# Post-LN transformer layer on one core: scores over all 128 array rows, heads' outputs to columns by DMA, and a new order of steps

## The reference

```python
qkv = (x @ Wqkv + bqkv)                      # 16 heads of width 16
scores = einsum('bhnqd,bhnkd->bhnqk', qb, kwin) / 16     # blocks of 128 queries, 384 keys
mask = (abs(kpos - qpos) <= 128) & (kpos >= 0) & (kpos < S)
attn = softmax(where(mask, scores, -1e30))
x = layernorm(x + (attn @ vwin) @ Wout + bout)
W1q, W2q = ternary(W1), ternary(W2)          # -1, 0 or 1
x = layernorm(x + relu(x @ W1q.T + b1) @ W2q.T + b2)
```

## Time and profile before

| | |
|---|---|
| median of 3 runs | 1186.8 us (1184.37 to 1189.89) |
| profiled execution, time | 1187.86 us |
| profiled execution, span | 1186.1 us |
| mean granted TensorE clock | 0.924 of 2.4 GHz |
| DMA moved | 81.49 MB |

### The profile page before, as it was taken

One profiled execution on the slowest core, in us unless ns is written; L12 is line 12 of the kernel. 1 busy time (PEld: TensorE's weight loads), 2 busy tenths in 40 slices (PEclk: granted clock), 3 DMA queues, 4 the chain that ended last, 5 costly groups with the idle time before them and its releaser, 6 DMA issues.

```text
span 1186.1 us, 23520 instructions
## 1 busy us (share of the span) xinstructions
PE 1056.2 (89%) x8132; PEld 771.9 (65%) x8132; DVE 859.3 (72%) x2934; ACT 613.3 (52%) x1258; POOL 518.8 (44%) x824
## 2 busy tenths in 40 slices
PE   4778899999989899998989999898989999897966
PEld 3444676766767576676767666676767667675755
DVE  3975777778787777778777777877777787777333
ACT  4154554655455564556455555545655554555421
POOL 2124353544535445463535445453535445344430
PEclk9677899998989999898999989898998989898889
DMA  5835255434354443444344534424554342442000
GB/s 169 108 54 92 28 82 82 68 70 73 58 75 68 83 73 76 61 80 65 56 82 73 88 61 78 75 37 82 82 82 68 69 74 57 57 69 56 1 19 18
DMA packets 56999, 81.49 MB, mean 69 GB/s; under 512 B 7729, under 2 KB 27697, under 8 KB 56882
## 3 DMA queue, kind: packets, MB, share of 16 engines
q1 hardware_dynamic: 56882, 80.00, 40.3%
HBM read 20.19 MB, written 8.39 MB: 24 GB/s over the span
## 4 chain that ended last, share of the span: by engine, by line
PE 77%; DVE 13%; issue 4%; POOL 2%; ACT 2%; DMA 1%; SPq 0%; POOLq 0%; DVEq 0%; ACTq 0%
PE shared L484 18%; PE st_a L459 13%; PE shared L503 12%; PE shared L595 11%; PE shared L582 10%; DVE mx L812 5%; PE st_b L459 5%; PE shared L578 3%; PE shared L564 3%; DVE oT_lo L859 2%; POOL ln_rstd L1007 1%; PE shared L543 1%; PE mx L475 1%; DVE qk_lo L839 1%; DVE rmax L812 1%
## 5 line engine op out<-in xcount | busy, mean ns | idle before, releaser
L812 DVE CUSTOM_DVE_ANT_0 mx<-mx,band 128x384 f32<-128x384 f32 (+1 forms) x1024 | 480.1, 514 | 187.0 <-PE mx L475 182.6
L670 ACT ACTIVATE probs<-st_a 128x384 f32<-128x384 f32 (+1 forms) x384 | 202.0, 526 | 371.3 <-PE st_a L459 367.7
L475 PE MATMUL mx<-k_stack,q_stack 48*128 48x384 f32 (+1 forms) x1024 | 273.0, 369 | 8.0 <-DMA k_stack<-qk_lo 3.9
L973 POOL TENSOR_SCALAR_AFFINE_SELECT probs<-probs 128x512 f32<-128x512 f32 (+1 forms) x256 | 128.8, 527 | 317.5 <-ACT probs L670 316.3
L670 ACT ACTIVATE probs<-st_b 128x384 f32<-128x384 f32 (+1 forms) x384 | 200.8, 523 | 0.0
L459 PE MATMUL st_a<-q_stack,k_stack 50*128 50x384 f32 (+1 forms) x512 | 186.9, 406 | 3.1 <-ACT probs L670 2.4
L475 PEld LDWEIGHTS mx<-k_stack,q_stack 48*128 48x128 f32 x1024 | 165.7, 201 | 13.2 <-DVE rmax L812 8.7
L503 PE MATMUL shared<-probs,v_aug 128*32 128x384 f32 (+1 forms) x2048 | 161.2, 445 | 0.7 <-DVE x L902 0.7
L459 PEld LDWEIGHTS st_a<-q_stack,k_stack 50*128 50x128 f32 x512 | 90.3, 197 | 104.2 <-issue 63.5
L812 DVE DVE_READ_ACCUMULATOR2_ANT rmax<- 128x1 f32 x1024 | 144.5, 141 | 0.0
L459 PE MATMUL st_b<-q_stack,k_stack 50*128 50x384 f32 (+1 forms) x512 | 143.2, 320 | 0.0
(11 more groups left out here) (107 smaller groups left out, 1965.3 us busy)
## 6 DMA issues: line engine op xcount, KB each, us to landing
q_stack<-qk_hi SPq DMA_DIRECT2D x128, 128.0 KB, 4.3
k_stack<-qk_hi SPq DMA_DIRECT2D x128, 128.0 KB, 5.2
x_raw<-in_xT SPq DMA_DIRECT2D x16, 512.0 KB, 5.7
q_stack<-qk_lo SPq DMA_DIRECT2D x64, 128.0 KB, 3.9
k_stack<-qk_lo SPq DMA_DIRECT2D x64, 128.0 KB, 5.5
y<-in_x SPq DMA_DIRECT2D x16, 512.0 KB, 6.1
out<-x SPq DMA_DIRECT2D x32, 256.0 KB, 2.1
probs<-in_w2T SPq DMA_DIRECT2D x1, 1024.0 KB, 10.6
```

The lines of the kernel that those rows point to most:

```text
L475: mm = pe.matmul(PMX[i % N_MAX][:, col:col + n], SQ[rows, hd, W * m:W * m + W], SK[rows, hd, k0:k0 + n], start=True, stop=True)
L670: act.activation(PR[:, v % 2, g // 2, lo:lo + n], PST[i % 2][:, 0:n], ACT.Exp, scale=SCALE) \
L812: mx = dve.tensor_tensor_reduce(ps, ps, band, 1.0, -3e38, ALU.add, ALU.max, RMAX[:, g, m:m + 1])
L973: pool.affine_select(out=pr_before, in_=pr_before, compare_op=ALU.is_ge, fill=0.0, base=0, pattern=[[0, n], [1, W]], channel_multiplier=-1)
```

## The change

- `scores` and `max_scores` use the array's rows 0 to 127 and 0 to 111. `SK` becomes two stacks, each with zeros where the other pair of quads has its q rows; the negated maxima and ones move to rows 124 to 127. Scores and maxima no longer lie in different halves.
- A stack transfer also waits for the maxima of quad v-2, and scores also wait for the stack of the quad two ahead. Scores get three banks, shared work two; `nmt` uses a maxima bank, and the next max unit in it waits for ScalarE's copy.
- `ut` and the `ot` transposes go. `columns` copies the even rows of `U` (o) to `OC` and the odd rows (its sums, 16 times each) to `SC` with two DMAs for each quad. A step `od` takes the reciprocal of 128x512 sums and multiplies, twice in a row: VectorE both reciprocals and one product, GpSimd the other product.
- The bias matmul of `f1` goes: ScalarE makes relu with bias in two instructions into `U` or `H32`, then a third copies to `HID[0]`; the low part comes from there, by VectorE, in one of four by GpSimd.
- First layer norm in two halves; three of four x1 tiles on ScalarE. `SIDE`, `LAG` and the weaving change; SP's order is the table `TRANSFERS`.

```diff
+SIDE = [
+    ["nmt", ("ot", 0), ("qk", 0), "pva", "pvb", ("vp", 0), ("qk", 1), ("od", 1)],
+    [("ot", 1), ("vp", 1), ("qk", 2), ("op", 0), ("ln1", 0), ("ln1", 1), ("op", 1), "nmt", ("ln1", 2), ("x1", 0),
+     ("x1", 1), ("ln1", 3), ("qk", 3), ("xs", 0), "pva", "pvb", ("x1", 2)],
+    [("x1", 3), ("x1t", 0), ("x1t", 1), "nmt", ("f1", 0, 0), ("f1", 0, 1), ("f1", 0, 2), ("f1", 0, 3), "pva",
+     "pvb", ("f2", 0)],
+    [("ln2", 0), ("xs", 1), ("f1", 1, 0), ("f1", 1, 1), ("od", 0), ("f1", 1, 2), ("ln2", 1), ("f1", 1, 3),
+     ("f2", 1), ("ln2", 2), "nmt", ("ln2", 3), "pva", "pvb", "xr"],
+BANKS = (3, 3)
+REST_ON_POOL = (1,)
+X1_ON_DVE = (0,)
+SCORES_AT = (0.31, 0.94)
+MAXIMA_AT = (0.47, 0.89)
+TRANSFERS = (('maxima', 0), ('stack', 3), ('columns', 0), ('stack', 0), ('x', 0), ('maxima', 1), ('columns', 1), ('maxima', 2), ('residual', 0), ('stack', 1), ('columns', 2), ('stack', 2), ('store', 0), ('maxima', 3), ('columns', 3), ('store', 1))
+LAG = {"ln1": 1, "ln2": 0, "qk": 0, "od": 1, "ot": 2, "x1t": 0, "f1": 1, "op": 0, "f2": 0}
+        units = [((i + SCORES_AT[0]) / UNITS * total * SCORES_AT[1], "scores", i) for i in range(UNITS)]
+        units += [((i + MAXIMA_AT[0]) / UNITS * total * MAXIMA_AT[1], "max", i) for i in range(UNITS)]
+                if not (first and v < 2):
+                    sp.wait_ge(s_mxf, 12 * (4 * r + v - 2) + 12)
+                    if v < 2 or stages(at)[2]:
+                        pe.wait_ge(s_stk[(v + 2) % 4], 96 * (b + v // 2) + 96)
-                    mm = pe.matmul(PST[i % 2][:, col:col + n], SK[rows, hd, W * m:W * m + W],
-                                   SQ[rows, hd, q0:q0 + n], start=True, stop=True)
+                    mm = pe.matmul(PST[i % N_SCORE][:, col:col + n], SK[c][:, hd, W * m:W * m + W],
+                                   SQ[:, hd, q0:q0 + n], start=True, stop=True)
-                rows = slice(64 * c, 64 * c + 48)
+                rows = slice(0, 112)
+                if i == NMT_AT[(v + 2) % 4] and not (first and v == 0):
+                    pe.wait_ge(s_nmt, 4 * r + v)
+                sp.dma_start(OC[rows, i, :], U[0:P:2, :]).then_inc(s_uin, 16)
+                sp.dma_start(SC[rows, :], U[1:P:2, :]).then_inc(s_uin, 16)
-                        pe.matmul(ps, B1[:, P * f:P * f + P], ONES2[:, :], start=True, stop=False)
+                    for k, f in enumerate((2 * p, 2 * p + 1)):
+                        last = act.activation(H[:, 256 * k:256 * k + 256], G[:, 256 * k:256 * k + 256], ACT.Relu,
+                                              bias=B1C[:, f:f + 1])
+                    act.wait_ge(s_hr, n + 1)
+                    act.activation(HID[0][:, 2 * p:2 * p + 2, :].rearrange("p f t -> p (f t)"), H[:, :],
+                                   ACT.Identity).then_inc(s_hh, 1)
+                    dve.wait_ge(s_uin, 128 * r + 64 * i + 64)
+                    dve.reciprocal(SC[:, :], SC[:, :]).then_inc(s_rc, 1)
+                    if i == 1:
+                        dve.tensor_tensor(OC[:, i, :], OC[:, i, :], SC[:, :], ALU.mult).then_inc(s_od, 1)
```

More of the change, by code:

```diff
@@ L106, in weave @@
         total = sum(COST.get(name_of(s), (0, 0))[0] for s in SIDE[v])
[L107 to L110, removed]
+        units = [((i + SCORES_AT[0]) / UNITS * total * SCORES_AT[1], "scores", i) for i in range(UNITS)]
+        units += [((i + MAXIMA_AT[0]) / UNITS * total * MAXIMA_AT[1], "max", i) for i in range(UNITS)]
+        units.sort()
         at, slot = 0, []
@@ L122, with units_before, ffn_steps_in_u @@
 WOVEN = weave()
+def units_before(v, step, kind):
+    return sum(k == kind for woven in WOVEN[v][:SIDE[v].index(step)] for _, k, _ in woven)
+NMT_AT = [units_before(v, "nmt", "max") for v in range(QUADS)]
+assert max(NMT_AT) < UNITS
+def ffn_steps_in_u():
+    out, n, last = [], 0, 0
+    for v in range(QUADS):
+        for step in SIDE[v]:
+            if name_of(step) == "f1":
+                n += 1
+                last = n if step[2] % 2 == 0 else last
+            if step == "pvb":
+                out.append(last)
+    return out
+U_FFN = ffn_steps_in_u()
 def stages(at):
@@ L179, in dve_order @@
                 due(maxima)
-        after = late[-1][0] + 1 if late and name_of(late[-1][1]) == name_of(step) in ("ln1", "ln2") else 0
+        after = late[-1][0] + 1 if late and name_of(late[-1][1]) == name_of(step) == "ln2" else 0
         late.append((max(maxima + LAG.get(name_of(step), 0), after), step))
@@ L412, in step @@
-                if post:
-                    store(b, 1)
+                for kind, v in TRANSFERS:
+                    if kind == "x" and nxt2:
+                        x_columns(b + 2)
+                        if at == -2:
+                            more_weights()
+                            zeros_and_ones()
+                    elif kind == "stack" and v == 3 and attn:
+                        stack(b, 3, at == 0)
+                    elif kind == "stack" and v < 3 and nxt:
+                        stack(b + 1, v, at == -1)
+                    elif kind == "store" and post:
+                        store(b, v)
+                    elif kind == "residual" and attn:
+                        residual(b)
+                    elif kind == "maxima" and row_of(v, "nmt", at) is not None:
+                        dr, vq = row_of(v, "nmt", at)
+                        maxima(b + dr, vq)
+                    elif kind == "columns" and row_of(v, "pvb", at) is not None:
+                        dr, vq = row_of(v, "pvb", at)
+                        columns(b + dr, vq)
@@ L751, in step @@
                             other_weights()
+                        row = row_of(v, step, at)
+                        before = name_of(step) in ("f1", "nmt", "ot", "pvb", "qk", "x1")
+                        if row is not None and before:
+                            side_work(v, step, b, *row, at)
                         for _, kind, i in woven:
@@ L754, in step @@
                                 exp(b, v, i, at)
-                        row = row_of(v, step, at)
-                        if row is not None:
+                        if row is not None and not before:
                             side_work(v, step, b, *row, at)
@@ L890, in side_work @@
                         .then_inc(s_x1l, 1)
-                elif name == "f1":
+                elif name == "f1" and step[2] not in REST_ON_POOL:
                     hf, p = step[1], step[2]
```

349 lines of the change are left out of this document (180 added, 169 removed), and 8 rows, old and new, of the table SIDE.

## The result

The changed kernel takes 1259.7 us (median, 1255.6 to 1263.0) beside 1186.0 of the kernel before: a ratio of 1.0615, interval 1.0572 to 1.0658. The forecast was 1117 (1060 to 1178) and faster; time, range and sign are all missed.

What follows compares the result with a forecast made beforehand. TensorE, busy 89% of the span, was taken to bound the kernel. Per row, -6.9 us of removed work and waits, -1.7 of half-rate clock and +4.1 of new waits gave -4.5: 63.7 us, 1117 us in all (1060 to 1178).

Steps and rivals of the forecast that it cites:

- a reciprocal holds the max units behind it for 2.8 us: VectorE's two reciprocals a row: max units wait, three banks cover most, TensorE loses +0.3 us twice a row.
- VectorE's 54.4 us: VectorE's forecast busy time a row, more than before in a shorter row, but under TensorE.
- The low clock: TensorE's half-rate stretch, 3.4 us a row, was to shrink to half: -1.7 us a row.
- rival 2: Low clock stays, or VectorE paces with reciprocals near 4 us: 66.2 us a row, 1155 us; chance 0.18.
- The bias matmuls: TensorE in f1: 16 matmuls of 0.118 us go, -1.9 us a row.
- ScalarE in `f1`: ScalarE needs 1.54 us plus an exp for a shorter TensorE step: +0.4 us a row in all.
- The scores over the full array: TensorE's scores and maxima one after another cost the same as paired half-array packs, 18.8 us a row: 0.
- rival 3: Pair worth more than its pack shows; padded 384-column matmuls at 0.28 us, +2.2 a row, 1218 us, slower; chance 0.07.
- The stack of quad 3: SP's queue: its transfers land 13 us into the row, scores and maxima wait: +1.0 us a row.
- The wait for x1: TensorE's wait before the x1 transposes, 1.7 us a row, was to stay, as tiles 2 and 3 hang on `op`.
- x1's low part: TensorE in f1, directly behind x1t, waits for the copy and difference: +1.2 us a row.
- at the head of the row: nmt comes first and the next max unit waits for ScalarE's copy from the same bank: +0.9 us a row.

Runs made afterwards that it cites:

- short: Changed kernel with each reciprocal taken of only 32 of its 512 columns, the other sums left undivided: 1140.1 us, ratio 0.960.
- pieces0: Changed kernel with only the first half's reciprocal cut into four of 128 columns, a max unit between each: 1263.8 us, ratio 1.063.
- hop0: Changed kernel with the first half's reciprocal taken of its 8 distinct rows as 128x32, then spread through DRAM, and its division later: 1206.3 us.
- bias_two: Kernel before with f1's bias matmuls replaced by two ScalarE relus with bias, low part from PSUM without bias: 1136.9 us, ratio 0.956.
- bias_act: Kernel before with the bias part alone: two ScalarE relus into an extra tile, a copy, low part from that tile: 1217.6 us, ratio 1.026.
- two: Changed kernel with two relus straight into HID[0], low part from PSUM without bias, GpSimd's low parts back on VectorE: 1303.5 us.
- short_two: Changed kernel with 32 of 512 columns inverted, two relus into HID[0], low part from PSUM without bias, GpSimd's low parts on VectorE: 1178.7 us.
- full_run1: Kernel before with full-array scores and padded stacks, units sent one by one instead of in runs of two: 1174.6 us, ratio 0.987.
- full_only: Kernel before with only the full-array scores, two padded stacks, their waits and shared tiles: 1175.4 us, ratio 0.990.
- pieces: Changed kernel with each reciprocal cut into four of 128 columns, a max unit between them: 1288.7 us, ratio 1.086.
- hop2: Changed kernel with both reciprocals as 128x32 spread through DRAM, second half's division later, its transfers ahead of the stack's: 1223.2 us, ratio 1.029.

## Why the prediction was wrong

1. **The step that failed** is the term "a reciprocal holds the max units behind it for 2.8 us; three banks cover most of that: +0.3 twice". It stood at 0.6 us a row; short measures it at 7.6. Four things are in it. The instruction is 3.34 us, not 2.8. It does not stand alone: the low part in front and the product behind make 4.65 us without maxima. The three banks cover 2.9 us of that (490.55 to 493.45), not the 3.9 that three units of 1.3 us would. And behind the first reciprocal it is not a max unit but the hidden layer's low part that is missed, which no bank covers. In the run the two waits are 67 us shorter in short (43.3 to 3.5 and 38.0 to 10.6), 4.5 us a row; the other 3.1 are the longer busy time, which goes with the low clock. The error behind all four: I compared VectorE's 54.4 us with a row of 63.7 and called it under TensorE. Busy time over a row says nothing of a stretch in which it is full (pieces0, hop0).
2. **The low clock** was to shrink by half. The granted clock of 0.95 stayed; in short it is 1.00, so this hung on point 1. My reading of where it fell in the kernel before was wrong too. The half-rate stretch starts at 344.7, behind the wait for `U` and ahead of the one for x1, which lies inside it; ahead of the fall stands one wait of 1.41 us, not the 3 us in 6 of rival 2:

```profile
343.81 0.30 PE L513 MATMUL shared<-identity,u 128*128 128x128 f32 x1 [1.41 <-ACT u L714]
...
346.61 1.73 PE L564 MATMUL shared<-identity,x 128*128 128x128 f32 x7 [1.15 <-ACT x L727]
```

In bias_two the wait for x1 is there (25.8 us in the run), the one for `U` is 1.0 us, and the clock is 1.00. Rival 2 had both mechanisms, low clock and reciprocals near 4 us holding maxima, and priced them 66.2 - 63.7 = 2.5 us a row above the forecast: right in kind, a third of the 7.6 in size.
3. **The bias matmuls**: -1.9 a row forecast, 68.23 - 64.88 = -3.35 measured alone. Distances between starts leave out what a shorter sequence gives back in waits and clock: the wait for `U` fell from 23.6 us to 1.0, and in bias_two's stretch of 360 to 428 us the granted clock is 1.00, against 0.95 in the earlier trace rows.
4. **ScalarE in `f1`**: +0.4 forecast. Against the two-instruction form the three-instruction form costs 5.7 us a row in the kernel before (bias_act, bias_two), and saves 3 in the new one (two, short_two, where GpSimd's share moved as well). I had weighed ScalarE's time, and not when the bank comes free nor that the low part reads two SBUF tiles.
5. **The scores over the full array**: 0 forecast. The 0.175 us is measured, and the part alone gives 1.0%, but outside the steady rows; in these it costs an estimated 2 to 3 us that the clock gives back (full_run1). So the pair was worth more than I had counted, in the direction of rival 3, whose price of 0.28 us for a padded matmul is out. By the rate that the Trainium skill gives for such tiles (TensorEngine Tiling (Array Packing), Theoretical Speedup: up to twice) the part would have added 9.4 us a row; no row of full_only or full_run1 shows that much.
6. **The stack of quad 3** on SP's queue, +1.0: it did not come. Its keys are in `k_stack_bottom`, for which TensorE never waits; the 6.5 us above are for `k_stack_top`, of quads 0 and 1, and lie ahead of 50 us. The wait for x1, forecast to stay, fell from 26.9 us to 15.4. Those for x1's low part (+1.2) and at the head of the row (+0.9) came as 16.0 and 5.8 us in the run, 1.1 and 0.4 a row.
7. With the reciprocals short the row is 65.2 where the forecast without them, without the stack and with a full clock, would be 63.7 - 0.6 - 1.0 - 1.7 = 60.4. The 2 to 3 us of point 5 may be part of these 4.8; the rest is not taken apart and stays open.

The split of the 7.6 us into 4.5 of waits and 3.1 of clock is read from the traces; no run kept these waits at a high clock.

## What to carry to other kernels

Before you call an engine's new work covered, look at the stretch in which it falls, not at its share of the row: take busy time by stretches of a tenth of a row and see which are full. Where one rare instruction stands in an engine's queue between the short ones that feed TensorE, add what stands directly in front of and behind it, and count the cover from the distances of TensorE's starts. When values are replicated for the sake of a layout, do the costly operation on them before the replication; and measure each part of a large change in the kernel in which it will run, since here one part changed its sign. Where a part's time comes out as forecast, look at the clock beside it: here a cost and a gain in clock hid each other.

## What was not expected of the hardware

- The reciprocal on VectorE is far slower than its other instructions: 3343 ns for 128x512, 938 for 128x128 (in pieces), 343 for 128x32, so 6.2 to 6.3 ns a column, where a product of 128x512 takes 0.69 us.
- A VectorE difference of two SBUF tiles (128x512), 0.69 us alone, took 1.51 us beside GpSimd's product (1.01 in the mean of its 64, 0.83 with that product gone); the form with one operand in PSUM took 687 ns in the mean of 128. The Trainium skill (SBUF — State Buffer, SBUF: two separate sides) says that a VectorE instruction with two SBUF inputs and a GpSimd one that reads SBUF exclude each other for a whole instruction. The trace agrees: the product ends at 463.93 + 1.26 = 465.19, and the difference, started at 464.23, ends 0.55 us behind it.
- GpSimd's power needs 81.9 us for 128x512; two columns take 0.72.
- A change between logarithm and exp on ScalarE costs 1.28 us each way.
- A transfer of 16 KB landed 5.0 us after its issue with a stack of 768 KB in front of it, and 1.4 with the stack behind it (hop2, 610.36 to 611.80); a spread of 256 KB was waited for 6.9 us with a stack behind it, and 3.6 without.
